# Two mixture-of-experts stages: every token through every expert, against tokens sorted by expert

## The reference, cut to what matters

```python
probs = softmax(x @ gate_w)                    # 4096 tokens, 8 experts
topk_probs, topk_idx = top_k(probs, 2)
h = gelu(x @ w1[expert] + b1[expert])          # 128 -> 512, for the token's two experts
y = h @ w2[expert] + b2[expert]                # 512 -> 128
out = sum(y * topk_probs)                      # over the two experts
```

## Time and profile before

| | us |
|---|---|
| median of 3 runs | 4935.69 (4932.38 to 4941.92) |
| the profiled execution: its own time | 4945.66 |
| its span, first to last instruction | 4943.9 |
| moe0, moe2, moe3 in the span | 874.4 to 1460.6, 3393.2 to 3906.2, about 4662 to the end |
| TensorE busy, VectorE, ScalarE, GpSimd | 76%, 52%, 44%, 21% of the span |

### The profile page before, as it was taken

How to read it: one execution, slowest core, us unless ns; L and a number is a source line. 1 busy time by engine, 2 the same in 40 slices (tenths; PEclk the granted TensorE clock), 3 DMA queues, 4 the chain that set the end, 5 groups by cost and what they waited for, 6 DMA issues and landing times. The chain is left out here.

```text
span 4943.9 us, 64940 instructions
## 1 busy us (share of the span) xinstructions
PE 3746.8 (76%) x19738; PEld 2542.2 (51%) x19800; DVE 2553.2 (52%) x6640; ACT 2187.2 (44%) x4248; POOL 1043.4 (21%) x1066
## 2 busy tenths in 40 slices
PE   3659955799976688868886888887999778720398
PEld 1227733477753366646553555554777556510266
DVE  5868845122224677647884444442222355589444
ACT  3446623233333288858884444442333333300132
POOL 1002211000000376637662000000000001154100
PEclk9779978799987599989998888988999866655599
DMA  1330020000000000000000000000000000000000
GB/s 37 67 65 5 9 69 26 39 0 0 0 11 10 18 1 1 0 18 1 1 0 16 1 0 0 0 0 34 1 0 0 5 0 0 0 2 0 18 0 17
DMA packets 45621, 58.54 MB, mean 12 GB/s; under 512 B 14058, under 2 KB 37836, under 8 KB 44588
## 3 DMA queue, kind: packets, MB, share of 16 engines
q1 hardware_dynamic: 38956, 50.63, 3.7%
q10 hardware_dynamic: 6528, 6.29, 0.9%
HBM read 34.87 MB, written 10.51 MB: 9 GB/s over the span
## 5 line engine op out<-in xcount | busy, mean ns | idle before, releaser
L418 PEld LDWEIGHTS bank<-moe_w,moe_hidden 128*128 128x128 f32 x5376 | 626.6, 192 | 78.7 <-issue 76.8
L418 PE MATMUL bank<-moe_w,moe_hidden 128*128 128x128 f32 x5376 | 630.3, 275 | 0.0
L408 PE MATMUL bank<-normed_t,moe_w 128*128 (+1 forms) x1344 | 615.6, 600 | 11.5 <-ACT moe_hidden L470 8.2
L470 ACT ACTIVATE moe_hidden<-bank,moe_b 128x512 f32<-128x512 f32 x544 | 372.8, 687 | 505.8 <-PE bank L408 504.3
L546 DVE SCALAR_TENSOR_TENSOR branch<-bank,moe_weights,branch 128x128 f32<-128x128 f32 x768 | 216.3, 345 | 707.8 <-PE bank L418 703.9
L90 POOL TENSOR_TENSOR branch_norm_shifted<-branch_norm_moments,eps 128x4 f32<-128x4 f32 x64 | 12.7, 198 | 1889.8 <-DVE branch_norm_moments L83 1889.8
L408 PEld LDWEIGHTS bank<-normed_t,moe_w 128*128 128x128 f32 x1344 | 244.9, 193 | 256.0 <-issue 240.0
L1987 POOL TENSOR_TENSOR local_size<-local_size,local_half_powers 128x8 f32<-128x8 f32 x128 | 257.0, 2008 | 203.3 <-DVE local_size L2053 199.2
L1691 PE MATMUL bank<-local_wqkv,local_shifted 128*128 128x512 f32 x384 | 211.2, 644 | 57.0 <-DVEq L2045 24.0
L1496 DVE TENSOR_TENSOR ssm_mixer<-ssm_decay,bank 128x384 f32<-128x384 f32 x256 | 133.2, 552 | 202.8 <-PE bank L1158 179.5
L1308 ACT ACTIVATE ssm_decay<-bank 128x384 f32<-128x384 f32 x256 | 120.3, 489 | 192.4 <-PE bank L1131 147.4
(11 more groups left out here) (530 smaller groups left out, 8432.7 us busy)
## 6 DMA issues: line engine op xcount, KB each, us to landing
rwkv_kept<-rwkv_keep SPq DMA_DIRECT2D x8, 768.0 KB, 11.8
moe_w<-in_moe_w_dram SPq DMA_DIRECT2D x2, 2304.0 KB
rwkv_gate<-rwkv_kept SPq DMA_DIRECT2D x8, 512.0 KB, 3.5
moe_w<-in_moe_w_dram SPq DMA_DIRECT2D x2, 2048.0 KB
rwkv_values<-rwkv_sent_v ACTq DMA_DIRECT2D x16, 128.0 KB
normed_t<-rwkv_sent_b SPq DMA_DIRECT2D x16, 128.0 KB
rwkv_recv<-rwkv_sent_r SPq DMA_DIRECT2D x16, 128.0 KB
x<-rwkv_sent_w ACTq DMA_DIRECT2D x16, 128.0 KB
```

The lines of the kernel that those rows point to most:

```text
L408: pe.matmul(hbank[n % 4][:], w1[:, e, f * P:(f + 1) * P], source_t[:, bass.ds(i * PN, PN)], start=True, stop=True).then_inc(hidden_up, 1)
L418: last = pe.matmul(obank[e % 2][:, t * P:(t + 1) * P], hid[:, e % 2, f, t * P:(t + 1) * P], w2[:, e, f, :], start=(f == 0), stop=(f == chu ...
L470: act.activation(hid[:, e % 2, f, :], hbank[n % 4][:], ACT.Gelu_apprx_tanh, bias=b1[:, n:n + 1] if bias else 0.0).then_inc(hidden_done, 1)
```

## The change

moe0 and moe2 no longer call `moe_block` but a new function `sorted_moe`:

- **Sorting.** The tokens are handled in two halves of 16 tiles. After the top two, two matmuls (`ranks`) and a chain of VectorE operations give each of a half's 4096 (token, expert) picks a slot, so that each expert's tokens lie together, padded to units of 128 rows. A half has 40 units (`UNITS`), 80 in all, always computed whether full or not. A table holds each unit's expert.
- **Scatter.** GpSimd issues 64 indirect DMAs (32 tiles, 2 picks), each of which writes 128 rows of 512 bytes of `normed` to their slots in DRAM. In moe0 the slots are first blanked: ten transfers of 512 KB on SyncE's queue, ahead of the load of the experts.
- **Units.** For each unit: SyncE loads 128 rows (64 KB), TensorE transposes them, ScalarE copies them out, VectorE copies the first layer's weights and bias of the unit's expert (128 x 516) to a fixed buffer, TensorE does `up` (four matmuls of 128 columns), ScalarE four gelus of 128 x 128, TensorE `down` (four matmuls, whose weights it reads at an address in a register), VectorE adds the bias, SyncE stores 64 KB to DRAM. VectorE reads the table into a register twice for each unit, TensorE once (`value_load`).
- **Gather and tail.** Once all units of a half are stored, GpSimd gathers each token's two rows (again 64 indirect DMAs in all), VectorE mixes them (8 operations a pair), and the tail follows. The four pairs of the first half are mixed in groups 6 to 9 of the units (a group is 8 units), those of the second half after the last unit.
- **moe0's shared expert** is computed ahead of the units, pair by pair, while the sorting and the scatter run.
- **Elsewhere.** The router of all three (also of moe3, still in `moe_block`) is now 32 matmuls with the tokens as weights and 8 columns moving, without turning and without ScalarE, and waits for the router's load alone. The blocks before moe0 and moe2 now also keep `normed` (`keep_rows=True`), 8 GpSimd copies in each.

The diff, cut to its core:

```diff
+def sorted_moe(core, name, tail, shared, normalised):
...
+            def turn(g, k):
...
+                pe.wait_ge(rows_loaded[k], (g + 1) * 16)
...
+                pe.transpose(tbank[k % 2][:, 0:UNIT], rows_in[:, k, :], core.ident[:]).then_inc(rows_turned, 1)
...
+            def up(g, k):
+                n = g * GROUP + k
+                pe.wait_ge(rows_taken, n + 1)
+                pe.wait_ge(record_ready, n + 1)
...
+                wait_from(pe, hid_done, n - 1)
+                for f in range(CH):
+                    last = pe.matmul(hbank[k % 2][:, f * UNIT:(f + 1) * UNIT], record[:, k % 4, f * P:(f + 1) * P],
+                                     rows_t[:, k % 2, :], start=True, stop=True)
+                last.then_inc(up_done, 1)
...
+            def down(g, k):
...
+                second = part_of_record(pe, n, W2, CH * C)
+                pe.wait_ge(hid_done, n + 1)
...
+                wait_from(pe, out_ready, n - 1)
+                for f in range(CH):
+                    last = pe.matmul(obank[k % 2][:, 0:C], hid[:, k % 2, f, :],
+                                     second[:, f * C:(f + 1) * C], start=(f == 0), stop=(f == CH - 1))
+                last.then_inc(down_done, 1)
...
+            for t in range(TILES):
+                for k in range(2):
+                    pool.indirect_dma_start(core.rows_dram[t // HALF_TILES][:, :], bass.IndirectOffsetOnAxis(ap=slots[:, k, t:t + 1], axis=0),
+                                            core.normed[:, t, :], None).then_inc(sorted_in[t // HALF_TILES], 16)
...
+            for h in range(HALVES):
+                for b in range(4):
+                    pool.wait_ge(outs_stored[b], 16 * (h + 1) * UNITS // 4)
+                for i in range(h * per_half, (h + 1) * per_half):
+                    gather(i)
+                    if i > h * per_half:
+                        tail.pool(pool, i - 1)
+                tail.pool(pool, (h + 1) * per_half - 1)
...
+            def fetch(g, k):
...
+                first_part = part_of_record(dve, n, 0, W2)
...
+                wait_from(dve, hid_done, n - 3)
+                dve.tensor_copy(record[:, k % 4, :], first_part).then_inc(record_ready, 1)
...
-            moe_block(core, "moe0", Tail(core, "moe0", keep_rows=False, turned=True), shared=True, bias=True,
-                      normalised=True, chunks=4)
+            sorted_moe(core, "moe0", Tail(core, "moe0", keep_rows=False, turned=True, bank=6), True, True)
...
-            moe_block(core, "moe2", Tail(core, "moe2", keep_rows=True, turned=False), shared=False, bias=True,
-                      normalised=False, chunks=4)
+            sorted_moe(core, "moe2", Tail(core, "moe2", keep_rows=True, turned=False), False, False)
```

More of the change, by code:

```diff
@@ L339, in moe_block @@
         hbank, obank, small = core.bank[0:4], core.bank[4:6], core.bank[6]
-        rbank = [small, hbank[3]]
-        loads = 3 + (2 if bias else 0) + (1 if shared else 0) + (2 if capacity else 0)
+        loads = 2 + (2 if bias else 0) + (2 if capacity else 0)
+        router_loads = 2 if shared else 1
         per_pair = heads * chunks
@@ L373, in _ @@
         def _(pe):
-            pe.wait_ge(weights_in, 16 * loads)
[L376 to L390, removed]
+            pe.wait_ge(router_in, 16 * router_loads)
+            for t in range(TILES):
+                last = pe.matmul(small[:, t * EXPERTS:(t + 1) * EXPERTS], source_t[:, t * P:(t + 1) * P], router[:],
+                                 start=True, stop=True)
+            last.then_inc(logits_up, 1)
+            pe.wait_ge(weights_in, 16 * loads)
             if capacity:
@@ L492, in _ @@
         def _(dve):
[L493 to L498, removed]
+            dve.wait_ge(logits_up, 1)
+            raw = small[:, 0:TILES * EXPERTS].rearrange("p (t e) -> p t e", e=EXPERTS)
+            if shared:
+                dve.wait_ge(router_in, 16 * router_loads)
+                dve.tensor_tensor(logits[:], raw, router_b[:].unsqueeze(1).broadcast_to([P, TILES, EXPERTS]),
+                                  ALU.add).then_inc(logits_down, 1)
+            else:
+                dve.tensor_copy(logits[:], raw).then_inc(logits_down, 1)
             dve.drain()
@@ L3349, in arrange, with records @@
     }
[L3351 removed]
+    def records(w1, w2, b1, b2):
         e, f, d = w1.shape
[L3354 to L3361, removed]
[L3362 to L3363 removed]
+        rows = [w1.transpose(2, 0, 1), b1.reshape(e, f // P, P).transpose(2, 0, 1),
+                w2.reshape(e, d, f // P, P).transpose(3, 0, 2, 1).reshape(P, e, f), np.broadcast_to(b2[None], (P, e, d))]
+        return np.concatenate(rows, axis=2)
+    step, segment = np.arange(UNITS, dtype=np.float32), np.arange(TILES * EXPERTS) % HALF_TILES > 0
+    expert = np.arange(HALVES * EXPERTS) % EXPERTS
+    rows = [out["earlier"], out["ones"]]
+    rows += [np.broadcast_to(v.astype(np.float32), (P, v.size)) for v in (step, segment, expert > 0)]
+    out["sort_tables"] = np.concatenate(rows, axis=1)
+    out["moe0_records"] = records(a["L0_ffn_spec_w1"], a["L0_ffn_spec_w2"], a["L0_ffn_spec_b1"], a["L0_ffn_spec_b2"])
+    out["moe0_own"] = records(*(a[f"L0_ffn_shared_{n}"][None] for n in ("w1", "w2", "b1", "b2")))[:, 0]
     out["moe0_router"] = a["L0_ffn_router_w"].T
[L3365 to L3366 removed]
+    out["moe0_router_b"] = np.broadcast_to(a["L0_ffn_router_b"], (P, EXPERTS))
+    out["moe2_records"] = records(a["L2_ffn_w1"].transpose(1, 0, 2), a["L2_ffn_w2"].transpose(1, 0, 2), a["L2_ffn_b1"],
+                                  a["L2_ffn_b2"])
     out["moe2_router"] = a["L2_ffn_gate_w"].T
[L3368 removed]
+    w1, w2 = a["L3_ffn_moe_w1"], a["L3_ffn_moe_w2"]
+    out["moe3_w1"] = w1.transpose(1, 0, 2)
+    out["moe3_w2"] = w2.reshape(EXPERTS, -1, P, C).transpose(2, 0, 1, 3)
     out["moe3_router"] = a["L3_ffn_router_weight"]
```

433 lines of the change are left out of this document (412 added, 21 removed).

## The result

| | us |
|---|---|
| median of 4 runs of the kernel before, beside it | 4936.88 (4932.38 to 4941.92) |
| median of 4 runs of the kernel after | 4775.5 (4770.26 to 4778.83) |
| ratio, 95% interval | 0.967, 0.9655 to 0.9689 |
| span of the profiled execution | 4777.0 (before 4943.9) |
| moe0 in the span | 873.8 to 1379.9: 506.1 (before 586.2, forecast 434) |

161 us are gained where 240 were forecast; the range (4470 to 4880) held the time, the likeliest time (4695) was 80 us low. 80.1 us came from moe0, 72.0 from moe2 and 10.3 from moe3's router (end of moe2 to the end of the logits: 781.7, then 771.4 us). About 5 us lie between moe0 and moe2, where nothing was forecast.

A forecast was written before the change was run, and what follows sets the result against it. TensorE was taken to bound moe0 and moe2. Gains of 78 us in moe2, 152 in moe0 and 11 in moe3, less 1 for copies, made 240 us: from 4935.7 to 4695 us, range 4470 to 4880.

The forecast's parts named there:

- First unit's transpose in moe2, 82 us into the stage: Start of moe2: sorting 29 us, 32 indirect DMAs 48, landing 2, first load and transpose 3.
- c: Time GpSimd needs per indirect DMA in scatter and gather: taken as 1.5 us.
- First unit in moe0, 83 us: Start of moe0: same chain as moe2, with the shared expert's 62 us hidden beside sorting and scatter.
- u: Period of one unit in the unit loop: 3.1 us, TensorE's work at 0.8 clock plus waits and half a register read.
- rival 1: Register reads hide, clock stays full: 2.2 us a unit, 2.7 in groups with a mix; 4530 us, chance 0.20.
- Groups 6 to 9, 31 us, bound by VectorE: Unit groups that also mix a pair: 8 x 2.6 + 10 = 31 us each on VectorE.
- 80 units, 273 us: All units of a stage: 48 at 3.1 us plus four groups at 31 us.
- End part, 78 us in moe0 and 80 in moe2: After the last unit: store, gathers of four pairs, GpSimd's tail steps, last mix and tail; 10 us before.
- moe3, 11 us: Gain from moe3's router alone, whose logits start after the router's load and end 11 us earlier.
- another wait in the unit loop: Unit loop: a stated sign that the forecast is wrong, such as rows late from DRAM or a store holding `outs`.
- Rivals 2 and 3: GpSimd bound, indirect DMA 2.5 us: 4823 us, chance 0.12; VectorE bound, register read 1.4 us: 4836 us, chance 0.10.
- rival 4: Slower than before: TensorE at 1.2 GHz in units, register read exposed, 5.5 us a unit; 5028 us, chance 0.10.

The follow-up runs named there:

- one_more: The kernel after with one more GpSimd instruction (additions to a spare semaphore) ahead of moe0's first scatter, on a fourth chip: 4611.6 us (0.934).
- copy_all: The kernel after with VectorE copying an expert's whole record per unit, so TensorE and the bias addition read no register: 4751.4 us (0.960).
- paced: The kernel after with each of the second half's 32 scatters waiting for one more finished unit: 4696.1 us (0.950).
- gathers: paced, plus first-half gathers each waiting for one more unit and GpSimd's norm steps put between gathers, on a third chip: 4602.6 us (0.931).
- late_own: The kernel after with TensorE held before pair 3 of moe0's shared expert until GpSimd has issued 28 scatters, third chip: 4631.4 us (one run).

## Why the prediction was right or wrong

The direction and the first part of the mechanism held: over two thirds of the expert work went (80 of 256 tile-expert products stay in a stage, where the prediction said three quarters), and sorting, units and end part came. By its steps, with the kernel after and, in brackets, one_more, whose work is the same and which is not held up:

- **First unit's transpose in moe2, 82 us into the stage**: 77.8 (77.6). c was 1.26 instead of 1.5, 8 us less; the logits took 13.8 instead of 10: 64 records at a granted clock of 0.50.
- **First unit in moe0, 83 us**: 167.6 (97.4). This is the step that failed. (By the prediction's own terms it should have been 88: the 6 us by which TensorE's order puts off the ranks are named and not added, and the scatter starts 42 us into moe0 in one_more, 34 into moe2.) "The shared expert's 62 us are thus hidden" was wrong twice. Undisturbed, a pair takes 9.4 us, not 7.0 to 8.2 (3.6 us for the first layer, 5.8 for the second, whose bias is a matmul of its own), and the last ends 97 us into the stage: 14 us are TensorE's even then. And beside the scatter it crawls, 70 us more.
- **Unit, u = 3.1 us**: 2.2 (2.2), with the granted clock at 1.00, not 0.8. VectorE stands idle for 0.8 us ahead of each copy, where its register read is, as priced, but beside TensorE's work; TensorE's own read costs at most 0.09 us (copy_all), not 0.4. This was rival 1's u, though not its 2.7 us a unit in the groups with a mix (3.4).
- **Groups 6 to 9, 31 us, bound by VectorE**: up to 36.0 (28, 27, 27 and 24). The bound was named rightly in the main and 4 us too long (in two such groups of one_more, 55 us, VectorE is busy for 27.3, stands ahead of its copies with "issue" for 12.5 and waits 9.7 for TensorE's results); gathers "covered" beside units were so in GpSimd's time, not in their effect on the others.
- **80 units, 273 us**: 258 in moe0 and 280 in moe2 (223 and 219).
- **End part, 78 us in moe0 and 80 in moe2**: 80.5 and 83.3 (80.7 and 83.5).
- **moe3, 11 us**: 10.3.

Together: without hold-ups the prediction's span (4943.9 - 240 = 4703.9) is 95 us above one_more's 4608.5: the units were 104 us too dear, the first units 10 and the end parts 6 too cheap, and 8 came outside the two stages (4 ahead of moe0, 3 between them). The hold-ups cost 4777.0 - 4608.5 = 168.5 us, 105 in moe0 and 61 in moe2. Two errors of opposite sign left 73 us in the span. That the time came out so near the forecast is luck: a unit priced too dear paid for a hold-up that nobody had thought of. Without the hold-up it would have been one_more's 4611.6, still inside the range. The second error is no mis-sized term. The prediction priced a transfer that it had no row for by the time of its own engine, and did not ask what it does to others; "another wait in the unit loop: rows that come late from DRAM, or a store that holds `outs`" looked at data alone. Rivals 2 and 3 fell with c and u, rival 4 with the clock, 1.00 through units 1 to 39.

## What to carry to other kernels

Price a new kind of instruction by what it does to the other engines too: look in the windows whether their busy time falls while it runs, with "issue" as the only releaser. Where it does, spread the indirect DMAs one to a step of the neighbouring work; paced did that at next to no cost to the units (2.24 in place of 2.22 us), and moe0's shared expert ended 83 us after the first scatter in place of 126. On a chip that holds nothing up there is nothing to gain by it: gathers took 4602.6 us and one_more, with everything dense, 4611.6. And before an edit is credited with a gain, run the unedited kernel on the same chip: here one_more's expected gain of 165 us came in as 164, and what another chip gave can't be told from what the edit gave.

## What the runs showed of the hardware

- An indirect DMA of 128 rows of 512 bytes takes GpSimd 0.96 us and 0.30 to the next, scatter or gather. A plain DMA of the same bytes takes it about 0.5 us (54 in 28.00 us).
- On two chips, and in the kernel after's own run, dense indirect DMAs hold TensorE to a quarter of its pace (17.1 us of work in 68), at 57 GB/s and a DMA share of 0.17, and ScalarE and VectorE too (in moe2 a gelu comes 28 us after its operand, a sum of VectorE 8.5); on two others the same instructions don't. Plain DMAs on the same queue don't either, at 142 and 102 GB/s.
- The hold-up does not begin with the burst: TensorE ran at full pace for its first 17.8 us, in straight-line code and in a loop alike, and in moe2, where it stood idle first, for 8 us from the 44th us of the burst on.
- It is no late block of instructions: TensorE's queue brought none between 915.2 and 1007.1 us, and its crawl ended at 1003 without one.
- When GpSimd had executed 16 indirect DMAs its sequencer had passed the 28th (late_own).
- TensorE's granted clock was 1.00 (2.4 GHz) through 87 us of units whose matmuls have 128 columns each, and 0.54 in the hold-up, near its lower level.
